# A four-layer graph network on one core: the sources and lanes of all edge tiles gathered ahead, and the attribute loads shared between two queues

## The reference

```
edge_index = jnp.stack([src, dst])
h = relu(layernorm(x));  x = x + mean over the edges into a node of (h[src] @ W + b)
h = relu(layernorm(x));  x = x + gated layer(h, edge_attr_32)
h = relu(layernorm(x));  x = x + filter layer(h, edge_attr_17)
h = relu(layernorm(x));  x = x + 3 normalised graph convolutions of h
```

## Time and profile before

| what | value |
| --- | --- |
| median of three runs | 8719.87 us (8703.91 to 8736.1) |
| the profiled execution | 8702.86 us |
| its span, first to last instruction | 8701.0 us |
| mean granted TensorE clock | 0.749 of full speed |
| busy share of the span | PE 67%, DVE 50%, POOL 37%, ACT 20% |
| instructions | 138050 |

### The profile page before, as it was taken

The page is one execution under the profiler, slowest core; times in us unless marked ns, Lnnn a source line. Parts: engine busy times, 40 slices in busy tenths (PEclk is TensorE's granted clock), DMA queues, the critical chain, the costliest instruction groups (busy, mean ns, idle before and its releaser), DMA issues. The chain is left out here.

```text
span 8701.0 us, 138050 instructions
## 1 busy us (share of the span) xinstructions
PE 5807.8 (67%) x29615; PEld 4088.1 (47%) x29617; DVE 4309.2 (50%) x14738; ACT 1723.7 (20%) x3202; POOL 3183.4 (37%) x3326
## 2 busy tenths in 40 slices
PE   4313666784455455555554688888888788889999
PEld 4312344663333333333332455555555555677777
DVE  7877888335666666666666333333333333332222
ACT  0013888101111111111111111111111111110000
POOL 0101000005555555555552455555555555300000
PEclk9956888897777777777777656655665666689999
DMA  1231333653333333333332211111111111256666
GB/s 31 101 100 60 105 106 107 215 180 77 68 71 69 70 70 67 71 69 70 71 70 31 42 34 35 34 35 34 35 34 34 33 36 35 24 188 252 249 243 221
DMA packets 1067041, 756.40 MB, mean 87 GB/s; under 512 B 870578, under 2 KB 979842, under 8 KB 1035091
## 3 DMA queue, kind: packets, MB, share of 16 engines
q1 hardware_dynamic: 679714, 476.62, 18.5%
q0 software_dynamic: 131296, 241.31, 10.9%
q10 hardware_dynamic: 255904, 37.09, 2.5%
HBM read 651.15 MB, written 141.61 MB: 91 GB/s over the span
## 5 line engine op out<-in xcount | busy, mean ns | idle before, releaser
L1883 POOL DMA_INDIRECT rows<-node_rows,idx_ring x1612 | 1529.2, 949 | 1215.1 <-DMA idx_ring<-src_all 702.5
L1883 POOL DMA_INDIRECT rows<-node_rows_wide,idx_ring x1612 | 1544.0, 958 | 1149.5 <-DMA idx_ring<-sorted_pairs 634.5
L1932 PE MATMUL ps_sum<-hots,act_ring 128*97 128x128 f32 x3224 | 657.8, 369 | 1326.6 <-DVE hots L1917 621.1
L1920 DVE TENSOR_SCALAR hots<-iota,lane_all 128x128 f32<-128x128 f32 x1612 | 461.6, 287 | 1820.4 <-remote 1283.4
L1932 PEld LDWEIGHTS ps_sum<-hots,act_ring 128*97 128x97 f32 x3224 | 556.7, 234 | 1618.9 <-DVE accT L1926 1235.1
L1932 PE MATMUL ps_sum<-hots,msg 128*96 128x128 f32 x3224 | 724.4, 399 | 419.0 <-DVE hots L1920 212.6
L1389 PE MATMUL ps_conv<-conv_rows,adj_ring 128*128 128x288 bf16 x7350 | 919.1, 287 | 29.8 <-PEq L1765 16.2
L1926 DVE TENSOR_TENSOR accT<-accT,ps_sum 97x128 f32 (+1 forms) x3224 | 905.8, 281 | 37.0 <-issue 16.0
L1932 PEld LDWEIGHTS ps_sum<-hots,msg 128*96 128x96 f32 x3224 | 624.9, 258 | 449.9 <-DVE accT L1926 360.2
L1959 PE MATMUL ps_e<-w1e,aT 128*128 128x384 f32 x1612 | 814.7, 642 | 18.3 <-DVE aT L1995 15.9
L1389 PEld LDWEIGHTS ps_conv<-conv_rows,adj_ring 128*128 128x128 f16 x7350 | 721.6, 98 | 212.1 <-issue 18.2
(11 more groups left out here) (345 smaller groups left out, 5907.2 us busy)
## 6 DMA issues: line engine op xcount, KB each, us to landing
adj_ring<-adjacency SPq DMA_DIRECT2D x240, 1280.0 KB, 5.5
adjacency<-panels SPq DMA_DIRECT2D x588, 128.0 KB, 1.7
attr_ring<-sorted_attr ACTq DMA_DIRECT2D x1612, 16.0 KB
idx_ring<-sorted_pairs SPq DMA_DIRECT2D x1612, 1.0 KB
rows<-node_rows_wide,idx_ring POOLq DMA_INDIRECT x1612
attr_ring<-sorted_attr SPq DMA_DIRECT2D x1612, 8.5 KB
rows<-node_rows,idx_ring POOLq DMA_INDIRECT x1612
sorted_attr<-in_edge_attr SPq DMA_DIRECT2D x5, 5000.0 KB
```

The source lines that it names most:

```text
L1883: g.indirect_dma_start(out=rows[:, r, j, 0:width], out_offset=None, in_=table, in_offset=bass.IndirectOffsetOnAxis(ap=idx, axis=0)).then_i ...
L1920: last = v.tensor_scalar(hots[:, r % 2, j, :], iota[:, :], lane, None, ALU.is_equal)
L1932: last = pe.matmul(ps_sum[0:M, r % 2, j, :], what(r, j), hots[:, r % 2, j, :], start=True, stop=True)
```

## The change

It has three parts.

**1. In the mean layer's block** all sources and targets are fetched at once. SP first spreads `tile_row` over 128 partitions (`tile_at`, 128 x 13). POOL then issues 13 gathers from `sorted_pairs`, each of 128 runs of 256 int32 (128 KB). ACT casts the 128 x 3328 integers to float32. PE transposes 26 pieces of 128 x 128, thirteen for the sources and thirteen for the targets, and ACT copies them out of PSUM in eight instructions into `src_all` and `lane_all`. In the `keep_wide` block one DVE instruction over 128 x 1612 subtracts `tile_node` from all lanes.

**2. In both edge passes** `idx_ring` is filled by ACT (`take_sources`, a copy of 128 x 4 from `src_all`) once the gathers of turn q - 6 are in. The pair loads, the index copy on SP, the waits on `fields` and `src_kept`, DVE's subtraction and ACT's `keep` are gone. POOL waits on `edge_used` of turn q - 6 as well.

**3. The attribute loads** of a turn are issued as two on SP and two on ACT in both passes. ACT's stages are in the order take_sources 0, load_half 0, tanh 5, gelu 4, and take_sources 0, load_half 0, keep_attrT 1, relu 2. In the filter pass PE's lags become 1, 2, 3 and 5 and DVE's 5, 6 and 4.

```diff
 mean_layer:
+                    sp.dma_start(tile_at[:, :], tile_row[:, :].rearrange("o (p k) -> o p k", k=TC))\
+                        .then_inc(tile_at_in.sem, 16)
                     load_adjacency(sp, ring, 0, range(1, NK))
+                    sp.wait_ge(tile_at_in.sem, 16)
...
                     gather_heavy(g, heavy_rows)
+                    g.wait_ge(tile_at_in.sem, 16)
+                    for k in range(TC):
+                        g.indirect_dma_start(out=pair_rows[:, k, :], out_offset=None, in_=pairs_h,
+                                             in_offset=bass.IndirectOffsetOnAxis(ap=tile_at[:, k:k + 1], axis=0))\
+                            .then_inc(pairs_in.sem, 16)
...
+                    a.wait_ge(pairs_in.sem, 16 * TC)
+                    a.activation(pair_rows[:, :, :].bitcast(F32).rearrange("p k e -> p (k e)"),
+                                 pair_rows[:, :, :].rearrange("p k e -> p (k e)"), ACT.Copy).then_inc(pairs_cast.sem, 1)
...
+                    def after(k, c, pair):
+                        if isinstance(k, int) and k == NK - 1 and c == 0:
+                            pe.wait_ge(pairs_cast.sem, 1)
+                            turn_pairs(0)
+                    multiply_panels(pe, ring, nodes, 3 * D + 2, ps, 0, (0,) * (NC - 1) + (1,), after)
+                    turn_pairs(1)
 edge_pass:
+                def load_half(a, q, turn, r):
                     past(a, rows_used, q - (GPI - 1))
-                    attributes(a, ACTE, q, r)
+                    attributes(a, ACTE, q, r, 1)
+                def take_sources(a, q, turn, r):
+                    if not isinstance(turn, int) or turn > 0:
+                        a.wait_ge(gathered[r].sem, base[gathered[r]] + turn * (16 * G))
+                        a.sem_inc(passed_a.sem, 1)
+                    a.activation(idx_ring[:, r, :], src_all[:, dyn(q * G, G)], ACT.Copy).then_inc(idx_ready[r].sem, 1)
...
                         past(sp, rows_used, q - (GPI - 1))
-                        if first:
-                            past(sp, src_kept, q - (GPI - 1))
-                            past(sp, fields, q - (GPI - 1))
-                            for j, row in enumerate(rows_of(q, SP)):
-                                sp.dma_start(idx_ring[:, r, j, :], pairs_h[dyn(row, P), :])\
-                                    .then_inc(idx_ready[r].sem, 16)
-                        else:
-                            sp.dma_start(idx_ring[:, r, :, 0], src_all[:, dyn(q * G, G)])\
-                                .then_inc(idx_ready[r].sem, 16)
-                        if kind == "filter":
-                            attributes(sp, SP, q, r)
+                        attributes(sp, SP, q, r, 0)
...
-                        g.wait_ge(idx_ready[r].sem, base[idx_ready[r]] + (turn + 1) * (16 * (G if first else 1)))
+                        g.wait_ge(idx_ready[r].sem, base[idx_ready[r]] + turn + 1)
                         g.sem_inc(gather_go.sem, 1)
+                        past(g, rows_used, q - (GPI - 1))
...
-                        turns(a, [(tanh, 5), (gelu, 4), (keep, 4),
-                                  (lambda q, t, r: load_attributes(a, q, t, r), 0)])
+                        turns(a, [(lambda q, t, r: take_sources(a, q, t, r), 0),
+                                  (lambda q, t, r: load_half(a, q, t, r), 0), (tanh, 5), (gelu, 4)])
```

More of the change, by code:

```diff
@@ L50 @@
 T = Q * G
+TC = -(-T // P)
 PIECES = 5
@@ L1492, in _, with turn_pairs @@
                     gather_heavy(g, heavy_rows)
+                    g.wait_ge(tile_at_in.sem, 16)
[3 more added lines that the diff above has]
+                            .then_inc(pairs_in.sem, 16)
+                @block.scalar
+                def _(a):
+                    a.wait_ge(pairs_in.sem, 16 * TC)
+                    a.activation(pair_rows[:, :, :].bitcast(F32).rearrange("p k e -> p (k e)"),
+                                 pair_rows[:, :, :].rearrange("p k e -> p (k e)"), ACT.Copy).then_inc(pairs_cast.sem, 1)
+                    for c, t in enumerate((src_all, lane_all)):
+                        by_run = t[:, :].rearrange("p (t n) -> p n t", n=TC)
+                        for n, (first, runs) in enumerate(quads):
+                            a.wait_ge(pairs_turned.sem, c * len(quads) + n + 1)
+                            a.activation(by_run[:, first:first + runs, :],
+                                         ps_p[:, n, 0:runs * P].rearrange("p (k t) -> p k t", t=P),
+                                         ACT.Copy).then_inc(pairs_kept.sem, 1)
                 @block.tensor
                 def _(pe):
-                    multiply_panels(pe, ring, nodes, 3 * D + 2, ps, 0, (0,) * (NC - 1) + (1,), lambda k, c, pair: None)
+                    def turn_pairs(c):
+                        for n, (first, runs) in enumerate(quads):
+                            if c:
+                                pe.wait_ge(pairs_kept.sem, n + 1)
+                            for k in range(runs):
+                                last = pe.transpose(ps_p[:, n, k * P:(k + 1) * P], pair_f[:, first + k, :, c], ident[:, :])
+                            last.then_inc(pairs_turned.sem, 1)
+                    def after(k, c, pair):
[4 more added lines that the diff above has]
+                    turn_pairs(1)
                 @block.vector
@@ L1824, in edge_pass, with rows_of, attributes @@
                 block = ctx.enter_context(nc.Block())
-                def rows_of(q, engine):
+                def rows_of(q, engine, half):
                     return nc.values_load_multi_w_load_instructions(
-                        tile_row[0:1, dyn(q * G, G)], [engine], min_val=0, max_val=PADDED,
+                        tile_row[0:1, dyn(q * G + half * (G // 2), G // 2)], [engine], min_val=0, max_val=PADDED,
                         skip_runtime_bounds_check_because="clamped to the last tile's row")[1]
-                def attributes(eng, engine, q, r):
-                    for j, row in enumerate(rows_of(q, engine)):
+                def attributes(eng, engine, q, r, half):
+                    for j, row in enumerate(rows_of(q, engine, half), half * (G // 2)):
                         if kind == "gated":
@@ L2051, in relu @@
                             a.activation(hid[0:D, r % 2, :], ps_e[0:D, r % 2, :], ACT.Relu).then_inc(edge_act.sem, 1)
-                        turns(a, [(lambda q, t, r: keep_attrT(a, q, t, r, KB, edge_mm), 0), (relu, 1)])
+                        turns(a, [(lambda q, t, r: take_sources(a, q, t, r), 0),
+                                  (lambda q, t, r: load_half(a, q, t, r), 0),
+                                  (lambda q, t, r: keep_attrT(a, q, t, r, KB, edge_mm), 1), (relu, 2)])
                     @block.vector
@@ L2061, in times @@
                                             ALU.mult).then_inc(edge_used.sem, 1)
-                        turns(v, [(lambda new, old: hots_and_adds(v, new, old), 4, 5), (times, 3)])
+                        turns(v, [(lambda new, old: hots_and_adds(v, new, old), 5, 6), (times, 4)])
                 for r in range(GPI):
                     uses = len(range(r, Q, GPI))
-                    idx_ready[r].n += 16 * uses * (G if first else 1)
+                    idx_ready[r].n += uses
                     attr_ready[r].n += 16 * uses * G
```

54 lines of the change are left out of this document (28 added, 26 removed).

## The result

The changed kernel takes 8800.56 us in the median (8773.95 to 8808.28) against 8713.41 us of the kernel before in the same comparison: a ratio of 1.0092, 95% interval 1.0073 to 1.0111. It is slower by 0.9%, where 7940 us had been forecast. Its profiled execution has a span of 8792.2 us, 91.2 more than the 8701.0 of before.

The account below looks back on a forecast made before the run. Both edge passes were taken as bound by a loop of waits, put down to index loads. Terms -510 (gated), -282 (filter), +5 (mean layer), +7 (lag) gave -780 from 8702.86: 7923, times 1.002, 7940 us; range 7340 to 8780.

Parts of the forecast that it names:

- The reading of the profile: Both edge passes: a loop of waits binds; turns of 6.67 and 6.80 us exceed POOL's 5.03 through index loads.
- rival two: Both edge passes: POOL issues continuously at its floor, 661 + 713 us gained, 7355 us in all; chance 0.14.
- The step that failed: Both edge passes: loads issued beside gathers crawl, delaying whatever waits for them; four SP attribute loads took 5.04 us against 1.52.
- the term of 1.27 us a turn for half the loads: Gated pass: half of DVE's 2.53 us idle a turn goes with half the loads, 510 us over 403 turns.
- Gated pass: Index loads gone and eight loads a turn cut to four: 510 us gained, bounds 330 and 661.
- ACT's copy: Gated pass: copying 128 x 4 numbers a turn runs beside ACT's other work, busy 109.53 of 600 us.
- a load on ACT at 0.60 us: Filter pass: two such loads lengthen ACT's turn by up to 1.2 us of 5.6 free, costed at nothing.
- Filter pass: Five loads a turn become four, two on SP and two on ACT: 0.70 us a turn, 282 us gained, bounds 143 and 428.
- The mean pass: Mean layer: 26 transposes on PE's path, 4.1 us, and one evacuation standing out at the end, together +5 us.
- the 7 us for one more lag: Filter pass: one more lag adds a turn of 6.8 us to its filling, +7 us.
- POOL's added wait on q - 6: Both edge passes: SP held the same wait for edge_used before loading the index, so no new condition.
- The fourth: Rival: gathers run too far ahead; filter pass 7.43 us a turn, gated gains nothing, slower at 8987 us; chance 0.15.

Follow-up runs that it names:

- e17: The changed kernel with POOL held to edge_used of turn q - 3 instead of q - 6 in the gated pass, second-kind chip: 7308.17 us (0.9995).
- e11: The changed kernel without attribute loads after the first six turns of each pass, first-kind chip: 8536.78 us.
- e12: The changed kernel without gathers after the first six turns of each pass, first-kind chip: 6247.42 us.
- e9: The changed kernel run again as it is, first-kind chip: 8784.41 us (1.0076).
- e2: The changed kernel with attribute loads issued as before, four on ACT (gated) or SP (filter), index copies still on ACT: 8688.87 us (1.0002).
- e4: The changed kernel with one attribute load a turn on SP in both passes, of the same bytes: 8623.99 us (0.9931).
- e10: The kernel of e2 with POOL held to edge_used of turn q - 3 in the gated pass, first-kind chip: 8509.34 us (0.976).
- e16: The kernel of e11 with POOL held to edge_used of turn q - 3 in the gated pass: 8458.94 us.
- e3: The changed kernel with one index copy on SP a turn instead of ACT's, attribute loads issued as before: 8780.59 us (1.0121).
- e1: The changed kernel with POOL held to edge_used of turn q - 3 instead of q - 6 in both passes: 8746.91 us (1.0068).
- e13: The kernel before with POOL also waiting for edge_used of turn q - 3 in the gated pass: 8561.17 us (0.9837).
- e14: The kernel of e2 with POOL held to q - 2 in the gated and q - 4 in the filter pass: 8747.1 us (1.0049).
- e15: The kernel of e2 with POOL held to q - 4 in the gated and q - 2 in the filter pass: 8731.05 us (1.0026).

## Why the prediction was wrong

**The reading of the profile held in its first half.** The passes are bound by a loop of waits, not by an engine, and POOL's floor is 5.03 us a turn: the chips of the second kind run at 5.00 to 5.04, and rival two's time, 7355 us, is within 0.7% of both e17 and the kernel before there. That is no merit of the change, which does nothing on those chips. That the index loads are where POOL's distance from its floor is booked was right; that it would go with them was not.

**The step that failed** is "hardware loads issued beside POOL's gathers crawl, and everything that waits for them crawls too", and with it the term of 1.27 us a turn for half the loads. The crawl is real, but it isn't what holds the pass. On chips of the first kind handoffs between engines come late while POOL issues gathers, with loads or without: tanh by up to 6.3 us in e11, DVE's one-hots by 8.2 in the stretch of the changed kernel. Without gathers they don't (e12). The crawl of register instructions in the earlier trace rows is one more thing that suffers, not the source, and it needs both: of such instructions (FUSED_REGOPS) 176 of 1228 take over 0.5 us on SP in the changed gated pass, 2050 to 4780, and none on SP, ACT or DVE in e12 (loads alone, first kind) or e17 (both, second kind), nor on ACT or DVE in e11 (gathers alone). With the crawl gone in e11, a turn still takes 6.53 us. Loads add something: 0.42 us a turn in the gated pass and 0.14 in the filter pass (e9 against e11), or 0.22 and 0.14 where they are issued as before (e2). With one load a turn the passes lie between, at 6.69 and 6.60 (e4); with the hold, loads add nothing to the gated pass (6.29 in e10, 6.32 in e16). Two issuers brought nothing here, and in the gated pass they cost 0.20 to 0.25 us a turn. The rule of the Trainium skill, page "DMA: Bandwidth & Descriptors", section "Issuing engines are not separate DMA queues", was nearer than my sum: it promises no more of a second issuer than the sequencer's time.

**Gated pass, forecast -510 us, measured +132.** By steps, over 403 turns: pair loads out, one copy on SP, 6.67 to 6.88, +85 us (e3); the copy on ACT instead of SP, to 6.75, -52 us (e2); the loads split, to 7.00, +99 us. I had costed ACT's copy at nothing, as a compute instruction of 0.19 us beside idle time, and a load on ACT at 0.60 us from the earlier trace rows, where two take 4.30 in the stretch above. The copy's place makes ACT's tanh and gelu, which wait on a DVE that is itself released late, the last link before POOL: 803.5 us of waiting. But that place is not shown to be the cost, for e3, with the copy on SP and not behind them, is slower than e2. The three steps are measured; why the first costs 85 us is open.

**Filter pass, forecast -282 us, measured -35.** The lags, with POOL's wait on q - 6, 6.80 to 6.75 (e3), index on ACT to 6.68 (e2), the split to 6.72. Each step is about as large as the 0.04 us by which the changed kernel's own two profiles differ.

**Smaller terms.** The mean pass was to cost 5 us, and the first gather is 5.4 later, but not for the reason given. The 13 gathers there were issued by 1609.09, and ACT turned to their transposes at 1900.14. The 26 transposes take 3.4 us of PE, where 4.1 were forecast. The product, from first to last matmul, takes 315.1 us for 306.0, and only 1.6 of the 9.1 are the transposes inside it: between 1604 and 1612, around the last of the gathers, PE stands still six times for 5.2 us, which I had put at nothing. In e17, on a chip of the second kind, the same product takes 306.7. No run isolates the 7 us for one more lag. POOL's added wait on q - 6 costs nothing in the gated pass, where none of POOL's idle time ends with it, and in the filter pass four waits, 15.2 us, do.

**The rivals.** The fourth, slower through long rows of gathers, had 0.15 and gave the sign, and rows of twelve at 7.1 us a turn, where I had seen 7.43. It put them in the filter pass, though, and its 8987 us is far above the 8801. Its mechanism, POOL running too far ahead, is not borne out: holds of two to four turns are alike, and e16 gains with its rows as long as before.

**What is shown and what is open.** Shown: a wait of POOL on `combine` two to four turns back takes 0.68 (e1), 0.27 (e13), 0.46 (e10) and 0.21 us (e16 against e11) off a gated turn, and a like wait on `times` puts 0.6 on a filter turn (e1, e14, e15). Open: whether it works because `combine` releases POOL directly and not through a chain of ACT or SP; why the sign turns in the filter pass; how a gather's issue delays the handoffs of others; and what makes a chip of one kind or the other. No run here tells these.

## What to carry to other kernels

A wait that is booked on a load says who came last, not who is slow: before costing its removal, look at whether the other engines' waits in the same stretch are long too. Here ACT's waits for z in the kernel before were up to 10.6 us long. A long wait is not yet a late handoff: set the start of the one that waits beside the end of what it waits for. To release the engine at the head of a loop by the event that it needs gained time in one pass and cost time in the other, so move such a wait in each pass by itself. And a kernel whose loop runs over many semaphores is to be timed on more than one chip: e10's 2.4% is 0.1% on another.

## What the runs showed of the hardware

The kernel before took 8689 to 8721 us on the chips of the first kind and 7311 to 7312 us on those of the second. The difference, 19%, is more than any edit gained or cost that left the gathers in. It is nearly all in the two passes with gathers: of the 1481.6 us between the spans of the changed kernel and e17, 1477.4 lie there. A turn takes 5.0 against 6.3 to 7.3 us, and without gathers the times are 6215 and 6247 us. A gather of 128 rows of 192 columns and one of 96 take the same 0.946 and 0.944 us to issue and 0.30 to the next, and a gated and a filter turn without loads take the same 6.53 and 6.54 us on the first kind, so nothing here is seen to depend on the bytes of a gather.

The late handoffs of e11 end when a row of gathers does: 108 of its 111 late starts of tanh come 1.5 us or more behind POOL's last gather. Work outside the passes is hit as well: the matmuls of the mean layer have six holes of 5.2 us in all beside 13 gathers on a chip of the first kind, and none on one of the second (e17). Whether these are late handoffs too, no run tells.
